# More probability chunks turned by way of DRAM, an earlier FFN input load and another PSUM bank in an attention and FFN kernel

## The reference

```python
x_norm = (x - mu) / sqrt(var + EPS) * gamma + beta
q, k, v = x_norm @ qkv[:, :512], x_norm @ qkv[:, 512:1024], x_norm @ qkv[:, 1024:]
attn = softmax(where(causal, q @ k.T / sqrt(512), -inf))
x1 = layernorm(x + (attn @ v @ o_proj + x))
p = softmax(x1 @ wr.T); routes, indices = top_k(p, 2); gates = routes / sum(routes)
h = silu(silu(x1 @ w1.T) @ w3.T) @ w2.T
ffn = zeros.at[indices[:, k]].add(gates[:, k] * h)
y = layernorm(x1 + ffn)
```

## Time and profile before

| | |
|---|---|
| median of 3 runs | 1644.82 us (1644.79 to 1644.96) |
| the profiled execution, own time | 1644.84 us |
| its span, first to last instruction | 1643.0 us |
| PE busy | 1616.7 us, 98% of the span |
| DVE, ACT, POOL busy | 886.3, 680.9, 285.1 us |
| granted TensorE clock, mean | 0.996 |
| idle of PE before `v` by probabilities | 14.2 us |

### The profile page before, as it was taken

How to read it: one execution, slowest core, us unless ns; L and a number is a source line. 1 busy time by engine, 2 the same in 40 slices (tenths; PEclk the granted TensorE clock), 3 DMA queues, 4 the chain that set the end, 5 groups by cost and what they waited for, 6 DMA issues and landing times. The chain is left out here.

```text
span 1643.0 us, 23601 instructions
## 1 busy us (share of the span) xinstructions
PE 1616.7 (98%) x7591; PEld 1338.3 (81%) x7591; DVE 886.3 (54%) x2296; ACT 680.9 (41%) x1301; POOL 285.1 (17%) x491
## 2 busy tenths in 40 slices
PE   9999999999999999999999999999979999999998
PEld 7888888888888888888888888888858888888886
DVE  5554645565364556546355545545556656656563
ACT  5443423354343344344333444333335444444442
POOL 1120201121120112121111212110131221212211
PEclk9999999999999999999999999999989999999999
DMA  4111635321153432124434212343554313223100
GB/s 160 58 65 54 153 82 134 93 97 56 55 141 96 118 95 97 64 72 127 113 96 110 84 60 95 103 122 106 138 123 70 51 26 51 32 44 51 26 0 8
DMA packets 365766, 136.64 MB, mean 83 GB/s; under 512 B 317008, under 2 KB 321104, under 8 KB 365664
## 3 DMA queue, kind: packets, MB, share of 16 engines
q1 hardware_dynamic: 354768, 116.48, 28.4%
q10 hardware_dynamic: 10896, 18.90, 3.7%
HBM read 79.73 MB, written 55.59 MB: 82 GB/s over the span
## 5 line engine op out<-in xcount | busy, mean ns | idle before, releaser
L351 PE MATMUL psum<-xt_hi,g_hi 128*128 128x512 f32 (+3 forms) x640 | 237.4, 371 | 0.4 <-DVE g_lo L920 0.4
L351 PE MATMUL psum<-v_hi,pt_hi 128*128 128x512 f32 x544 | 221.3, 407 | 14.2 <-DVE pt_lo L931 11.8
L353 PE MATMUL psum<-xt_lo,g_hi 128*128 128x512 f32 (+3 forms) x640 | 229.6, 359 | 0.0
L352 PE MATMUL psum<-xt_hi,g_lo 128*128 128x512 f32 (+3 forms) x640 | 229.2, 358 | 0.0
L352 PE MATMUL psum<-v_hi,pt_lo 128*128 128x512 f32 x544 | 213.6, 393 | 0.0
L353 PE MATMUL psum<-v_lo,pt_hi 128*128 128x512 f32 x544 | 213.4, 392 | 0.0
L508 POOL TENSOR_TENSOR var_eps<-meanvar,eps 128x2 f32<-128x2 f32 (+1 forms) x97 | 19.1, 197 | 1000.0 <-DVE meanvar L898 997.8
L943 DVE TENSOR_REDUCE rowmax<-psum 128x1 f32<-128x512 f32 (+3 forms) x160 | 97.0, 607 | 148.6 <-PE psum L353 147.2
L818 ACT ACTIVATE act_f<-psum 128x512 f32<-128x512 f32 x128 | 76.5, 598 | 200.0 <-PE psum L353 200.0
L639 ACT ACTIVATE tok<-tok,shift,rstd 128x512 f32<-128x512 f32 x128 | 97.5, 808 | 109.3 <-POOL shift L513 109.0
L351 PEld LDWEIGHTS psum<-v_hi,pt_hi 128*128 128x128 f32 x544 | 102.7, 189 | 41.1 <-DVE pt_lo L931 17.5
(11 more groups left out here) (149 smaller groups left out, 3403.1 us busy)
## 6 DMA issues: line engine op xcount, KB each, us to landing
xin<-in_x ACTq DMA_DIRECT2D x64, 256.0 KB, 2.8
tok<-in_x SPq DMA_DIRECT2D x64, 256.0 KB, 2.7
x_scratch<-tok SPq DMA_DIRECT2D x64, 256.0 KB, 2.2
out_dram<-tok SPq DMA_DIRECT2D x64, 256.0 KB, 2.3
p_scratch<-probs SPq DMA_DIRECT2D x64, 256.0 KB, 2.0
probs<-p_scratch SPq DMA_DIRECT2D x256, 64.0 KB, 2.5
x_in<-x_scratch SPq DMA_DIRECT2D x64, 256.0 KB, 4.2
p_scratch<-probs SPq DMA_DIRECT2D x16, 192.0 KB, 1.9
```

Source lines behind the costliest of these rows:

```text
L351: pe.matmul(o, ws, ms, start=first, stop=False, skip_group_check=True)
L352: pe.matmul(o, w_lo, ms, start=False, stop=False, skip_group_check=True)
L353: return pe.matmul(o, ws, m_lo_, start=False, stop=last, skip_group_check=True)
```

## The change

The far set becomes a list of chunks: tiles 3, 7 and 8 to 14 whole, and chunks 1 to 3 of tile 15. PE's transposes of these go, and SP and DVE get stores, loads and transposes for them. Bank 3 takes the second input unit of every group but the first. In the last batch SP loads the first FFN group behind the loads of tile 15's chunks 1 and 2, ahead of the stores of tiles 13 and 12; DVE's wait for it moves from ahead of chunk 2 to behind it; and the norm of tile 14 moves behind the split of the first FFN group, on POOL behind the FFN's memsets.

```diff
-    FAR = range(2 * GROUP, TILES - 1)
+    FAR = [(t, c) for t in range(TILES) for c in range(chunks(t)) if (t in (GROUP - 1, 2 * GROUP - 1) or 2 * GROUP <= t < TILES - 1 or t == TILES - 1 and c >= 1)]
...
-        SPARE = 2
+        SPARE = 3
         def x_bank(g, u):
-            return SPARE if g == 1 and u == 1 else XBANK
+            return SPARE if g and u == 1 else XBANK
...
# SP, tile(b, t)
-                if t in FAR:
-                    for c in range(chunks(t)):
-                        store_p(b, t, c)
-                    for c in range(2):
-                        load_p(b, t, c)
+                far_parts = [c for c in range(chunks(t)) if (t, c) in FAR]
+                for c in far_parts:
+                    store_p(b, t, c)
+                for c in far_parts[0:2]:
+                    load_p(b, t, c)
+                if t == TILES - 1 and last:
+                    sp.wait_ge(scores_ready, B * CHUNKS)
+                    for i in range(SLOTS):
+                        sp.wait_ge(x1_stored[i], 2 * GROUP // SLOTS * DMA)
+                    load_x1(sp, 0, 0)
...
# POOL and ACT: the norm of tile 14 in the last batch
-                if t and t != TILES - 2:
+                if t and t != TILES - 2 and not (t == TILES - 1 and last):
                     norm_behind(b, t - 1, z=2 if before or t > 1 else 1)
...
                 pool.memset(buffer[:].bitcast(F32), 0.0).then_inc(zeros_ready, 1)
+            norm_behind(B - 1, TILES - 2)
...
                 round_x1(0, c)
+            norm_behind(B - 1, TILES - 2)
             norm_behind(B - 1, TILES - 1)
...
# DVE, tile(b, t)
-                if t in FAR:
+                if (t, 0) in FAR:
                     turn_probs(b, t, 0)
...
-                if t == TILES - 1:
-                    norm_behind(b, t - 1)
+                if t == TILES - 1 and not last:
+                    norm_behind(b, t - 1)
+                if t == TILES - 1:
+                    if (t, 2) in FAR:
+                        turn_probs(b, t, 2)
+                    split_probs(b, t, 2)
                 if t == TILES - 1 and last:
                     dve.wait_ge(x1_loaded[0], LOADS)
                     turn_x1(0, 0)
                     turn_x1(0, 1)
-                if chunks(t) > 2 and t not in FAR:
-                    split_probs(b, t, 2)
-                if t == TILES - 1 and last:
-                    turn_x1(0, 2)
-                    turn_x1(0, 3)
...
+                if t == TILES - 1:
+                    if (t, 3) in FAR:
+                        turn_probs(b, t, 3)
                     split_probs(b, t, 3)
...
                 if t == TILES - 1 and last:
+                    turn_x1(0, 2)
+                    turn_x1(0, 3)
                     split_wr()
...
                     split_first_x1()
+                    norm_behind(b, TILES - 2)
                     residual(b, TILES - 1)
```

More of the change, by code:

```diff
@@ L230, in attention_mlp @@
                 TURNS += [("v", t + 1 + j) for j in range(GROUP)]
-            if t not in FAR:
-                TURNS += [("p", t, c) for c in range(chunks(t))]
+            TURNS += [("p", t, c) for c in range(chunks(t)) if (t, c) not in FAR]
         def turn_use(t, c):
@@ L362, in load_x1 @@
                                  rows_of[q]).then_inc(x1_loaded[slot], DMA)
-        NEAR_CHUNKS = [(t, c) for t in range(TILES) if t not in FAR for c in range(chunks(t))]
-        FAR_CHUNKS = [(t, c) for t in FAR for c in range(chunks(t))]
+        NEAR = [(t, c) for t in range(TILES) for c in range(chunks(t)) if (t, c) not in FAR]
         def near(b, t, c):
-            return b * len(NEAR_CHUNKS) + NEAR_CHUNKS.index((t, c)) + 1
+            return b * len(NEAR) + NEAR.index((t, c)) + 1
         def far(b, t, c):
-            return b * len(FAR_CHUNKS) + FAR_CHUNKS.index((t, c)) + 1
+            return b * len(FAR) + FAR.index((t, c)) + 1
         def through_dram(b, t, c):
-            tiles_with = [u for u in FAR if chunks(u) > c]
+            tiles_with = [u for u, part in FAR if part == c]
             return b * len(tiles_with) + tiles_with.index(t) + 1
@@ L425, in store_out, with tile @@
                 sp.dma_start(out[bass.ds(b * S + t * P, P), :], tok[:, t % SLOTS, :]).then_inc(out_stored[t % SLOTS], DMA)
-            def tile(b, t, before=True):
+            def tile(b, t, before=True, last=False):
                 slot = t % SLOTS
@@ L444, in tile @@
                     store_out(b - 1, TILES + t - 3)
-                if t in FAR:
-                    for c in range(2, chunks(t)):
-                        load_p(b, t, c)
+                for c in far_parts[2:]:
+                    load_p(b, t, c)
             for t in range(3):
@@ L456, in _ @@
             for t in range(3, TILES):
[L457 to L462, removed]
+                tile(B - 1, t, last=True)
+            load_x1(sp, 1, GROUP * P)
             for t in range(TILES - 2, TILES):
@@ L663, in wait_turned @@
             def wait_turned(b, t, c):
-                if t in FAR:
+                if (t, c) in FAR:
                     act.wait_ge(far_probs_turned, far(b, t, c))
@@ L692, in turn_probs @@
                 w = width(t, c)
-                turned_ = pt_f[:, n % 2, 0:w] if t in FAR else psum[:, turn_bank(turn_use(t, c)), 0:w]
+                turned_ = pt_f[:, n % 2, 0:w] if (t, c) in FAR else psum[:, turn_bank(turn_use(t, c)), 0:w]
                 act.activation(pt_hi[:, n % 2, 0:w], turned_, ACT.Copy).then_inc(pt_hi_ready, 1)
@@ L753, in tile @@
                     norm_x(b + 1, 0)
-                if t and t != TILES - 2 and not (t == TILES - 1 and not last):
+                if t and t < TILES - 2:
                     norm_behind(b, t - 1, (0, 1) if before or t > 1 else (0,))
@@ L993, in tile @@
                     split_probs(b, t, 0)
-                if t in FAR:
+                if (t, 1) in FAR:
                     turn_probs(b, t, 1)
@@ L1016, in tile @@
                     split_x(b + 1, 0, 2)
-                if t in FAR:
+                if t != TILES - 1:
                     for c in range(2, chunks(t)):
-                        turn_probs(b, t, c)
+                        if (t, c) in FAR:
+                            turn_probs(b, t, c)
                         split_probs(b, t, c)
@@ L1040, in tile @@
                     turn_x1(0, 1)
-                if chunks(t) > 2 and t not in FAR:
-                    split_probs(b, t, 2)
-                if t == TILES - 1 and last:
-                    turn_x1(0, 2)
-                    turn_x1(0, 3)
                 if t == TILES - 1 and not last:
                     split_g(b + 1, 0)
-                if chunks(t) > 3 and t not in FAR:
+                if t == TILES - 1:
+                    if (t, 3) in FAR:
+                        turn_probs(b, t, 3)
                     split_probs(b, t, 3)
```

## The result

The changed kernel takes **1648.05 us** (median; runs from 1644.5 to 1651.2), the kernel before 1645.45 (1644.1 to 1646.7): ratio 1.0015, interval 1.0009 to 1.0021. Forecast were 1638.6 us and a range up to 1643.0. It is slower by 2.6 us, where 6.2 us less were expected. The profiled execution took 1647.96 us, with a span of 1646.2.

What follows compares the result with a forecast made beforehand. The prediction took PE's own work to bound the kernel. Its terms, +1.4 + 0 - 1.8 - 2.8 - 3.0 = -6.2 us from the profiled execution's 1644.84, gave 1638.6 us; the forecast was 1636.5 to 1641.4, the range 1634.0 to 1643.0.

Steps and rivals of the forecast that it cites:

- What a transpose is worth: On PE, a block of four transposes costs 0.46 us, so the 24 blocks taken off give at most 11.0 us.
- Tile 3, +1.4: Tiles 3 and 4, every batch: DVE's transpose stands behind tile 4's first maximum, PE starts later; 0.35 us lost a batch.
- The bank, 0: Tile 4: the new bank removes PE's 0.5 us wait, but DVE's split bounds the second chunk; 0 us (-2.2 to 0).
- Tile 7, -1.8: Tile 7: 0.9 us won in each of batches 0 and 3, nothing in 1 and 2; -1.8 us (0 to -3.7).
- Tile 15, -2.8: Tile 15, batches 0 to 2: chunk 1 gives nothing, chunks 2 and 3 give 0.46 us each; -2.8 us.
- The last batch, -3.0: Last batch: PE reaches the FFN 7.1 us earlier, then waits for ACT; the end gains 3.0 us (0 to -7.1).
- ACT's chain behind tile 15's statistics: Last batch: PE waits for ACT in the first FFN group, so the end sees this chain: -3.0 us, not 7.1.
- the clock falls after each new wait: Rival: tile 3's 1.2 us gap slows some 12 products by 0.2 us in each batch; +9.6, 1648.2 us; chance 0.03.
- a low clock outside the last batch: Sign that the prediction is wrong: the clock is low anywhere but in the last batch.
- DVE waiting for loads by more than 1 us: Sign that the prediction is wrong: DVE waits more than 1 us for loads of probabilities.

Runs made afterwards that it cites:

- e1: The changed kernel with 20 instead of 14 warming products at the very start, which moves PE's code on: 1640.58 us.
- e10: e8 with tile 3 through DRAM again, DVE's transpose of it ahead of the residual and of tile 4's first maximum, and 20 warming products: 1629.26 us.
- e8: e7 with tile 7 turned on PE again as well: 1630.57 us.
- e4: The changed kernel with tile 3 turned on PE again: 1640.21 us.
- e6: e7 with the old bank for the second input unit: 1631.28 us.
- e7: e4 with the last batch's tile 15 turned on PE again and ACT's normalisation of tile 13 behind its rounding of chunk 2: 1631.89 us.
- e9: e8 with tile 15 turned on PE in every batch: 1635.12 us.
- e2: The kernel before the change with 9 instead of 14 warming products, which moves PE's code back: 1650.47 us.

## Why the prediction was wrong

**The step that failed** is in the part on tile 7: "In batches 1 and 2 DVE itself starts late (2.69 us "issue" at the loop's return ...)". I read that row as DVE's own matter and as fixed, and the sum has no term, no bound and no rival for PE's return to the same loop. It was 0.37 us before, and I took that for its price, when it was the price at one place of the code. The change takes a block of transposes out of the code ahead of the loop, the head moves back by 9 instructions, and each return costs 3.75 us (e1 against the change): 7.5 us. Without them the changed kernel takes 1640.6 us, faster by 0.3% and inside the forecast range; this one step decides the sign and most of the miss.

The account by terms: read at the same products before and after, PE loses 1.3 us at tiles 3 to 6, wins 1.7 at tile 7 in batches 0 and 3 and 2.3 at tile 15 in batches 0 to 2, loses 8.2 at the two returns with tile 7 behind them, and wins 2.3 in the last batch. Together that is 3.2 us lost, the difference of the spans.

The other steps:

- **What a transpose is worth.** Held: in e10 tile 3 wins 0.41 to 0.47 us a batch on e8 by the traces, where 0.46 was read for four.
- **Tile 3, +1.4.** The mechanism held: the new wait is 1.2 to 1.3 us in each batch, and DVE's order makes it (e10). So did the size: the 1.3 us above. (With tile 3 alone taken back, e4 against e1, it is 0.5 to 0.6 us a batch.)
- **The bank, 0.** Held (e6), and for the reason given: in e7 PE comes to tile 4's first chunk 0.7 us earlier than in e6, and to its second at the same time.
- **Tile 7, -1.8.** Wrong in size. Batches 0 and 3 held: 0.85 us each, where 0.9 was forecast. In 1 and 2 PE comes to the chunk at 454.07 in e1, where I wrote 454.1, but "nothing won" was read off against the old time of 453.94. In e1 PE came to the tile 0.3 us ahead by what the tiles before had won, and lost 0.4 in that wait, in each of the two. By the traces 0.9 us are left (0.7 by e7 against e8), too little to show in the times.
- **Tile 15, -2.8.** Held within 0.5 us (2.3 by the traces of before and after; 3.3 by the spans of e9 and e8). No load came late in batches 0 to 2 by more than PE had to spare.
- **The last batch, -3.0.** By the traces -2.3: PE is 5.5 us late against the old trace ahead of it and 3.2 at the end. Of the waits I gave, 4.1 for chunk 2 was 3.95, but chunk 1's load landed 1 us later (1.15 for 0.2), and chunk 3's wait of 3.3 became 0.27, as PE did chunk 2 at half clock (12 products in 4.9 us, from 1210.1 on), which the prediction allowed for. That ACT's chain behind tile 15's statistics is what the end sees was only half right: PE does wait for ACT's rounding of h (0.4 us) and for DVE's splits of it (0.7 and 1.5), but in e7, with the x1 load issued earlier, the chain moves up with the rest.

The rival "the clock falls after each new wait" gave 1648.2 us, the time that came, and was wrong: behind the wait of 1.29 us at tile 3 the clock is 1.00. After, the stretches 388.2 to 389.9 and 389.9 to 393.0 us:

```profile
388.20:389.90 1.70, 0.41 (x5) 0.24 (x3) 0.92 (x3) 0.63 (x1) 0.00 (x0) 1.00 0.00 0
389.90:393.00 3.10, 3.10 (x14) 2.57 (x15) 2.77 (x12) 1.13 (x4) 0.41 (x3) 1.00 0.02 5
```

It fell behind the two returns and, as the sum allowed for, behind the long wait of the last batch. Of the signs of being wrong that the prediction named, two came: a low clock outside the last batch, and DVE waiting for loads by more than 1 us (2.01 and 2.40 us in the last batch, above).

What stays open: what e7's two edits and the x1 load are worth each, and why the runs of the changed kernel spread over 6.7 us where those of the one before spread over 2.6.

## What to carry to other kernels

A loop's return is a term of the sum. When a change adds or removes instructions anywhere ahead of a loop's head, look for gaps marked "issue" at the return on the engine that bounds the kernel, count the packets of its code queue there, and try the same kernel with its code moved by some 20 instructions before you judge the change; 7.5 us of this verdict were that. Second, when a transfer is moved ahead, look at what else the same change puts into that queue: here the last batch's order was worth some 10 us (e9), the change got 2.3 of them, and eleven new issues (three stores, eight loads) stood ahead of the load that it had moved up. Third, gains ahead of a wait that another engine sets are lost in it; compare with what PE reaches after the other terms, not with the old time.

## What the runs showed of the hardware that I had not expected

- PE's code came in packets of some 16 KB. At the first return the second was asked for 3.1 to 3.3 us behind the first in every run looked at (443.50 and 446.56 in the change, 444.35 and 447.50 in e2), and the products that needed it started 2.9 and 2.7 us later (449.44 and 450.21).
- Where products were left to cover it the second fetch cost nothing: 0.2 to 0.4 us at the return in the kernel before, e1 and e4.
- Behind the gap of 3.3 us the granted clock fell to 0.50 some 1.3 us after products had begun again; behind the gap of 1.75 in e2 it stayed at 1.00. At half clock some nine products cost another 1.6 us (PE's lag on e1 grows from 3.4 us at the sixth product of the head to 4.95 at the fifteenth).
- One warming product of the code (`ident` by `ident`, float32) was two products and two weight loads in the trace, 28 for 14; a transpose (`ident` and `probs`, float32) was one of each.
